# Two tiles in a step of a two-layer graph attention kernel, with the turned activations moved to the projection banks

## The reference

```python
def layer(x, adj, l):
    q, k, v = projections(x, l)                    # 384x384 each, float32
    if l == 0:
        s = q @ k.T / sqrt(32) + beta * adj        # -9e15 where adj <= 0
    else:
        s = q @ k.T * 384 ** -0.5 + adj            # a row that is all zero gives zero
    o = softmax(s) @ v
    return o if l == 0 else o @ Wo.T + bo
x = layernorm(x + layer(x, adj, 0))
x = layernorm(x + layer(x, adj, 1))
```

## Time and profile before

| | us |
|---|---|
| median of 3 runs | 1067.73 (1065.7 to 1071.74) |
| the profiled execution | 1066.61 |
| its span, first to last instruction | 1064.8 |
| PE busy | 1035.8 (97%) |
| DVE busy | 793.6 (75%) |
| POOL busy | 788.6 (74%) |
| ACT busy | 451.0 (42%) |
| chain that ended last | PE 89%, DVE 3%, POOL 3% |

### The profile page before, as it was taken

The page is one execution under the profiler, slowest core; times in us unless marked ns, Lnnn a source line. Parts: engine busy times, 40 slices in busy tenths (PEclk is TensorE's granted clock), DMA queues, the critical chain, the costliest instruction groups (busy, mean ns, idle before and its releaser), DMA issues.

```text
span 1064.8 us, 38493 instructions
## 1 busy us (share of the span) xinstructions
PE 1035.8 (97%) x16896; PEld 898.1 (84%) x16896; DVE 793.6 (75%) x1578; ACT 451.0 (42%) x717; POOL 788.6 (74%) x646
## 2 busy tenths in 40 slices
PE   6999999999999999999999999999999999999985
PEld 5888888888888888888888888888888888888874
DVE  3587886868778687786868778687786868877884
ACT  4454434444344443444445344443434444444332
POOL 1588777778687786877778777777877867777676
PEclk9999999999999999999999999999999999999998
DMA  6421112112111121111211021121111210010100
GB/s 205 142 71 52 34 44 66 40 44 62 40 44 39 44 62 44 40 46 39 67 44 52 33 59 39 44 62 44 39 47 36 62 44 10 17 37 10 35 32 31
DMA packets 61750, 53.33 MB, mean 50 GB/s; under 512 B 35984, under 2 KB 55440, under 8 KB 61584
## 3 DMA queue, kind: packets, MB, share of 16 engines
q1 hardware_dynamic: 60752, 49.69, 15.9%
q10 hardware_dynamic: 832, 1.18, 0.3%
HBM read 38.28 MB, written 12.58 MB: 48 GB/s over the span
## 4 chain that ended last, share of the span: by engine, by line
PE 89%; DVE 3%; POOL 3%; issue 2%; DMA 1%; ACT 1%; POOLq 0%; SPq 0%; DVEq 0%
PE ps_u L374 53%; PE ps_h L374 9%; PE ps_s L392 8%; PE ps_s L464 8%; PE ps_h L486 7%; PE ps_h L410 2%; PE ps_h L498 2%; POOL probs L806 1%; DMA xt_in<-in_x_t 1%; DVE row_sum L716 1%; ACT probs L597 1%; DVE probs L675 1%; DVE row_max L684 1%; POOL probs L812 0%; POOL xt_lo L832 0%
## 5 line engine op out<-in xcount | busy, mean ns | idle before, releaser
L806 POOL TENSOR_TENSOR probs<-probs,row_max 128x768 f32<-128x768 f32 x128 | 193.2, 1510 | 223.2 <-DVE row_max L684 223.2
L812 POOL TENSOR_TENSOR probs<-probs,row_inv 128x768 f32<-128x768 f32 x128 | 193.2, 1509 | 2.8 <-DVE row_inv L720 2.5
L716 DVE TENSOR_REDUCE row_sum<-probs 128x12 f32<-128x768 f32 x128 | 122.0, 953 | 68.0 <-ACT probs L597 68.0
L559 ACT COPY probs_t<-ps_s 128x768 f32<-128x768 f32 x128 | 102.8, 803 | 109.9 <-PE ps_s L464 109.8
L374 PE MATMUL ps_u<-w_hi_v,xt_lo 128*128 128x384 f32 x384 | 137.7, 359 | 0.0
L374 PE MATMUL ps_u<-w_hi_v,xt_hi 128*128 128x384 f32 x384 | 129.4, 337 | 0.0
L374 PE MATMUL ps_u<-w_lo_v,xt_hi 128*128 128x384 f32 x384 | 129.1, 336 | 0.0
L684 DVE TENSOR_REDUCE row_max<-probs 128x12 f32<-128x768 f32 x128 | 121.4, 948 | 2.2
L374 PE MATMUL ps_u<-xt_hi,w_lo_q 128*128 128x512 f32 x285 | 121.6, 427 | 0.0
L597 ACT ACTIVATE probs<-probs 128x768 f32<-128x768 f32 x128 | 108.6, 849 | 28.9 <-POOL probs L806 27.0
L374 PE MATMUL ps_u<-xt_hi,w_lo_k 128*128 128x512 f32 x288 | 118.2, 410 | 0.9 <-ACT q_sb L585 0.9
(11 more groups left out here) (80 smaller groups left out, 2102.6 us busy)
## 6 DMA issues: line engine op xcount, KB each, us to landing
x_in<-in_x SPq DMA_DIRECT2D x16, 768.0 KB, 4.6
out<-z SPq DMA_DIRECT2D x64, 192.0 KB, 1.9
xt_in<-in_x_t SPq DMA_DIRECT2D x15, 768.0 KB, 4.7
adj<-in_adj SPq DMA_DIRECT2D x64, 128.0 KB, 3.0
xt_in<-in_x_t SPq DMA_DIRECT2D x3, 256.0 KB, 4.4
q_sb<-in_wq ACTq DMA_DIRECT2D x3, 192.0 KB, 4.6
k_sb<-in_wk ACTq DMA_DIRECT2D x1, 576.0 KB, 7.4
v_sb<-in_wv SPq DMA_DIRECT2D x1, 576.0 KB, 7.3
```

The source lines that it names most:

```text
L559: nc.scalar.copy(probs_t[:].rearrange("p (a i) n -> p a (i n)", a=2), ps_s[:, 0:2, 0:KT * P]).then_inc(probs_t_ready, 1)
L716: nc.vector.reduce_sum(row_sum[p][:], probs[p][:].rearrange("p i b k -> p (i b) k"), AX_X)\
L806: nc.gpsimd.tensor_tensor(s, s, over_keys(row_max[p]), ALU.subtract).then_inc(shifted, 1)
L812: nc.gpsimd.tensor_tensor(s, s, over_keys(row_inv[p]), ALU.mult).then_inc(probs_ready, 1)
```

## The change

- `slots` lets the turns (phases) 2 to 27, 26 of the 32, run in two steps of two tiles; the others keep four steps of one. `cur`, `prev` and `last` are now groups of tiles, j being the place (0 or 1) in the group. `last` is still the group of two steps before, so it is now up to a turn back.
- Scores of the second tile go to the other half of the same ps_s banks; heads of the second tile to the next columns of ps_h; turned probabilities of tile j to banks 2j and 2j+1 of ps_s, and to a buffer `probs_t[j]` each; the result of tile j to bank j of ps_h. `probs` and the row statistics have four buffers instead of two.
- The turned activations are numbered among the units (kind "x", `columns`) and use the two ps_u banks. A step of layer 1 thus puts its early unit, two x units and its late units through the two banks.
- `heads_out` and `heads_lo` handle both tiles in one instruction.
- ACT, DVE and POOL have a new order in a step (below).
- The o1 weights are staged in the memory of adj1, without a staging buffer of their own; SP stores behind its loads.
- The first products: ten matmuls of the identity (`warm_up`), then `first_units`, two units at once, high by high first; the scores of the very first tile wait for one q and k unit at a time, and in phase -1 the early unit is copied out ahead of the activations.

```diff
+def slots(phase):
+    if 2 <= phase <= N_TURNS - 5:
+        return [(0, 1), (2, 3)]
+    return [(0,), (1,), (2,), (3,)] if phase < N_TURNS else [(0,), (1,)]
...
-UNIT_ORDER = [u for s in STEPS for u in s.units]
+UNIT_ORDER = [u for s in STEPS for u in early(s) + columns(s) + late(s)]
...
# PE
+            def bank_free(no):
+                if no > 2:
+                    freed = UNIT_ORDER[no - 3]
+                    if freed[2] == "x":
+                        pe.wait_ge(xt_lo_ready[1], low_no((*freed[:2], freed[3])))
+                        return
...
+            def turn_activations(unit):
+                layer, c, _, t = unit
+                no = UNIT_NO[unit]
+                pe.wait_ge(normed, at((0, c, t)) + 1)
+                bank_free(no)
+                for g in range(KT):
+                    last = nc.tensor.transpose(ps_u[:, (no - 1) % 2, g * P:(g + 1) * P],
+                                               x1[c % 3][:, t, g * P:(g + 1) * P], ident[:])
+                last.then_inc(unit_made, 1)
...
+            def warm_up():
+                for _ in range(WARM_UP):
+                    nc.tensor.matmul(ps_h[:, 0, 0:P], ident[:], ident[:], start=True, stop=True)
+            def first_units():
+                last = [None, None]
+                for g in range(KT):
+                    pe.wait_ge(first_hi, 2 * g + 2)
+                    for n in range(2):
+                        nc.tensor.matmul(ps_u[:, n, :], w_hi["q0"][:, g, n * P:(n + 1) * P], xt_hi[0][:, g, :],
+                                         start=(g == 0), stop=False)
+                    pe.wait_ge(first_lo, 2 * g + 1)
...
+            warm_up()
+            first_units()
             for s in STEPS:
-                if s.cur:
-                    scores(s.cur)
+                for j, tile in enumerate(s.cur):
+                    scores(tile, j, s)
                 for unit in early(s):
-                    make_unit(unit)
-                if s.last:
-                    result(s.last)
-                if s.turned:
-                    turn_activations(s.turned, s.last)
-                if s.prev:
-                    turn_probs(s.prev, s.cur)
+                    if UNIT_NO[unit] > 2:
+                        make_unit(unit)
+                for j, tile in enumerate(s.last):
+                    result(tile, j, s)
+                for unit in columns(s):
+                    turn_activations(unit)
+                for j, tile in enumerate(s.prev):
+                    turn_probs(tile, j, s)
                 for unit in late(s):
-                    make_unit(unit)
-                if s.prev:
-                    heads(s.prev, s.turned)
+                    if UNIT_NO[unit] > 2:
+                        make_unit(unit)
+                for j, tile in enumerate(s.prev):
+                    heads(tile, j, s)
...
# ACT
+                for unit in early(s):
+                    unit_out(unit)
                 if place == (-1, 1):
                     for t in range(TILES):
                         activations_hi((*ORDER[1], t))
-                for unit in early(s):
+                if s.phase >= 0:
+                    for tile in s.turned:
+                        activations_hi(tile)
+                for j, tile in enumerate(s.prev):
+                    probs_out(tile, j, s)
+                for tile in s.cur[:1]:
+                    exponentials(tile)
+                for unit in late(s)[:1]:
                     unit_out(unit)
...
+                for tile in s.cur[1:]:
+                    exponentials(tile)
+                for unit in late(s)[1:]:
+                    unit_out(unit)
...
# DVE
+                for j, tile in enumerate(s.cur):
+                    add_bias(tile, j, s)
+                for tile in s.cur[:1]:
+                    maxima(tile)
...
+                if s.phase >= 0:
+                    for tile in s.turned:
+                        activations_lo(tile)
+                for j in range(2):
+                    for tile in s.last[j:j + 1]:
+                        residual(tile, j)
+                    if len(s.ts) == 2:
+                        for unit in late(s)[j:j + 1]:
+                            unit_out(unit)
+                for tile in s.cur[1:]:
+                    maxima(tile)
+                for tile in s.cur[:1]:
+                    sums(tile)
+                for unit in late(s)[2 if len(s.ts) == 2 else 0:]:
+                    unit_out(unit)
+                for tile in s.cur[1:]:
+                    sums(tile)
...
# POOL
+                for tile in s.cur[:1]:
+                    shift(tile)
...
+                if s.phase >= 0:
+                    for tile in s.turned:
+                        add_bo(tile)
+                        activations_lo(tile)
+                for tile in s.cur[1:]:
+                    shift(tile)
+                for j in range(2):
+                    for tile in s.last[j:j + 1]:
+                        inverse_deviation(tile)
+                        normalise(tile)
+                    for tile in s.cur[j:j + 1]:
+                        scale(tile)
```

More of the change, by code:

```diff
@@ L36 @@
 FIRST_AT = [[0, 1], [2, 3], [4, 5], []]
-Step = namedtuple("Step", "phase t cur prev last done turned units")
+Step = namedtuple("Step", "phase ts cur prev last turned units")
 def at(tile):
@@ L56, in units_of_step, with columns @@
     return out
+def slots(phase):
+    if 2 <= phase <= N_TURNS - 5:
+        return [(0, 1), (2, 3)]
+    return [(0,), (1,), (2,), (3,)] if phase < N_TURNS else [(0,), (1,)]
 def schedule():
     steps = []
-    attended = {}
+    groups = [(), ()]
     for phase in range(-1, N_TURNS + 1):
[L63 to L70, removed]
+        for ts in slots(phase):
+            groups.append(tuple((*ORDER[phase], t) for t in ts) if 0 <= phase < N_TURNS else ())
+            turned = tuple((*ORDER[phase + 2], t) for t in ts) if phase + 2 < N_TURNS else ()
+            units = [u for t in ts for u in units_of_step(phase, t)] if phase < N_TURNS else []
+            steps.append(Step(phase, ts, groups[-1], groups[-2], groups[-3], turned, units))
     return steps
 STEPS = schedule()
+def columns(s):
+    return [(*tile[:2], "x", tile[2]) for tile in s.turned if tile[0] == 1]
 def early(s):
@@ L396, in scores @@
                 last.then_inc(scores_made, 1)
[L398 to L414, removed]
-                layer, c, kind, n = unit
-                p, no = home((layer, c)), UNIT_NO[unit]
+            def bank_free(no):
                 if no > 2:
                     freed = UNIT_ORDER[no - 3]
+                    if freed[2] == "x":
+                        pe.wait_ge(xt_lo_ready[1], low_no((*freed[:2], freed[3])))
+                        return
                     if freed[2] == "v" and freed[:2] == ORDER[-1]:
@@ L424, in make_unit @@
                         pe.wait_ge(qk_ready, QK_NO[freed])
+            def turn_activations(unit):
[7 more added lines that the diff above has]
+                last.then_inc(unit_made, 1)
+            def make_unit(unit):
+                layer, c, kind, n = unit
+                p, no = home((layer, c)), UNIT_NO[unit]
+                bank_free(no)
                 w = f"{kind}{layer}"
@@ L471, in heads @@
                 pe.wait_ge(probs_t_ready, at(tile) + 1)
-                if at(tile) > 0:
-                    pe.wait_ge(z_ready, at(tile))
-                if turned and turned[0] == 1:
-                    pe.wait_ge(xt_lo_ready[1], low_no(turned))
+                if s.last:
+                    pe.wait_ge(z_ready, at(s.last[-1]) + 1)
                 if (layer, c) == ORDER[-1]:
@@ L712, in sums @@
             def sums(tile):
-                layer, c, t = tile
-                p = t % 2
+                layer, c, p = tile
                 dve.wait_ge(exp_ready, at(tile) + 1)
@@ L802, in shift @@
             def shift(tile):
-                p = tile[2] % 2
+                p = tile[2]
                 pool.wait_ge(max_ready, at(tile) + 1)
@@ L817, in add_bo @@
                     return
-                pool.wait_ge(xt_made, second_no(tile))
+                pool.wait_ge(unit_made, UNIT_NO[layer, c, "x", t])
                 if second_no(tile) == 1:
```

241 lines of the change are left out of this document (116 added, 125 removed).

## The result

The changed kernel takes 1151.65 us (median of 4 runs, 1150.1 to 1158.42), the kernel before 1067.2 in the same measurements: a ratio of 1.080 with a 95% interval of 1.077 to 1.083. The forecast was 1081, with 1097 as the upper end of its range. The profiled execution took 1150.36 us, its span is 1148.4.

A forecast was written before the change was run, and what follows sets the result against it. The prediction took TensorE as the bound, busy 99.99 of 100 us. Pairs of turns added 15.6 and the start took off 2.0: 1066.6 + 15.6 - 2.0 = 1080.2, or 1081 for the median; range 1060 to 1097.

The forecast's parts named there:

- The seams: TensorE's changes of kind of work: two tiles share each, saving 0.47 us a step, 24 us over 13 pairs.
- a pair: Two turns, eight one-tile steps becoming four: 62.3 us of TensorE work, 65.6 with waits, against 64.4 before.
- The wait in A: TensorE waits 2.9 us for the fourth late unit's bank: 1.8 from the step's own chain, 1.1 from D's lateness.
- step A: Layer 1, tiles 0 and 1, with layer 0 results and four late q/k units: 15.6 us without waits.
- the two instructions that make the next bias, 1.2: VectorE's last work in D's chain, from 16.8 to 18.0, making VectorE enter A at 2.5 instead of 1.38.
- B: Layer 1, tiles 2 and 3, with four late v units: 13.6 us, no stall.
- C: Layer 0, tiles 0 and 1, with four late q/k units: 17.5 us, plus a 0.4 wait for GpSimd's second scale.
- D: Layer 0, tiles 2 and 3, with four late v units: 15.5 us, handing lateness on to A.
- The start: Warm-up products, new first-unit order and earlier evacuation: first scores about 2.6 us earlier, -2 us, bounds 0 and -4.
- rival 4: Seams not saved, or GpSimd's late second scale also delays C's fourth late unit: 1088 to 1105, chance 0.23.
- half the waits, 1.6 a pair: Part of the rival that TensorE is fed all the same (chance 0.10): waits of A and C halved, 1062.
- waits of 2.5 to 4 a pair: The forecast's own case for TensorE's waits over two turns: 1074 to 1088, chance 0.50.

The follow-up runs named there:

- the waits away: Changed kernel with heads before the last late unit, VectorE's second-tile maxima early and its order by layer, held v unit evacuated last: 1065.2 us, 0.997 of before.
- the kernel with single steps: The changed kernel with one tile in every step and all the rest of the change kept: 1064.8 us, 0.997 of before.
- heads first: The changed kernel with the heads of both tiles made before the last late unit in two-tile steps: 1098.4 us, 1.027 of before.
- scores twice: The kernel before, with TensorE making every tile's scores twice into the same place: 1190.3 us, 1.113 of before.
- 42 warm-up products: The changed kernel with 42 warm-up products instead of 10 at the front of TensorE's stream: 1156.6 us.
- the order mended: The 1065.2 us kernel (heads before last late unit, VectorE reordered, held v unit out last), plus step C's early unit between its two tiles' scores: 1058.0 us, 0.991.
- VectorE's maxima early: The changed kernel with the second tile's maxima ahead of both residuals and the first two v units on VectorE: 1116.7 us, 1.044 of before.

## Why the prediction was wrong

The sign was right, the size was not: +14 forecast, +84.5 measured, outside the range. The sign was not luck: the waits that the forecast reckoned are there, and without the stops the ledger below comes to about 1094, inside the range.

- **The seams: right.** 96 scores take 1.21 us to the next projection matmul (254.53 to 255.74), where two groups of 48 take 1.42; two heads groups take 1.17. No switch is paid between tiles. With the waits away a pair fell to 62.9, against 62.3 reckoned.
- **The wait in A: right in place, too small by 1.0.** The changed kernel, VectorE, GpSimd, ScalarE and TensorE in step A, which begins at 254.53:

```profile
256.35 1.84 DVE L688 SCALAR_TENSOR_TENSOR bias<-adj,beta_col,bias 128x512 f32<-128x512 f32 x1
258.12 1.94 DVE L717 TENSOR_TENSOR probs<-ps_s,adj_both 128x384 f32<-128x384 f32 x4
...
266.68 0.94 DVE L729 TENSOR_REDUCE row_max<-probs 128x12 f32<-128x768 f32 x1
```

```profile
256.00 1.64 POOL L873 TENSOR_TENSOR probs<-probs,row_inv 128x768 f32<-128x768 f32 x1
```

```profile
269.21 0.84 ACT L633 ACTIVATE probs<-probs 128x768 f32<-128x768 f32 x1 [3.67 <-POOL probs L867]
269.96 0.67 ACT L623 ACTIVATE k_sb<-ps_u,k_bias 128x512 f32<-128x512 f32 x1
```

```profile
260.20 0.85 PE L496 MATMUL ps_s<-ident,probs 128*128 128x128 f32 x6 [0.72 <-DVE probs L717]
...
261.87 0.55 PE L496 MATMUL ps_s<-ident,probs 128*128 128x128 f32 x3 [0.82 <-POOL probs L873]
...
270.68 0.50 PE L389 MATMUL ps_u<-xt_hi,w_lo_k 128*128 128x512 f32 x1 [1.79 <-ACT k_sb L623]
```

  The fourth late unit starts at 16.15 in A, released by ScalarE's evacuation behind the exponential; forecast was 15.15. VectorE began the bias of A at 3.6, not 2.5. The term that was off is "the two instructions that make the next bias, 1.2": the second took 1.84 us here, 0.82 in the mean of the earlier trace rows, which is 15 times 0.75 and once 1.84. Before the turned probabilities there are two waits where the forecast had one, of 1.45: 0.7 us for VectorE's bias and 0.8 for GpSimd's scale. A took 19.6 for 18.5; B, C and D 13.6, 17.7 and 15.4 for 13.6, 17.9 and 15.5.
- **The start: right.** The first scores come at 20.0 (23.2 before); turn 2 begins 1.8 us earlier, and the kernel with single steps is 0.3% faster than before, about 2 to 3 us.
- **The step that failed** is the sum itself: "Two tiles in a step go through each seam once" was costed as a gain only. I took the 0.01 us from one small matmul to the next as good for any length of the group. What the runs showed in its place: in and right behind a burst of 384 small instructions there are stops of 46.6 us, and the lower clock after them, for which the sum had no term. The ledger, from the step lengths of the two profiled executions (spans of 1148.4 and 1064.8, so 83.6 us):

| | us |
|---|---|
| 13 pairs at 66.3 instead of 64.4 | 25.4 |
| the 21 stops | 46.6 |
| the three shorter stops in the early unit | 2.5 |
| the lower clock | 17.1 |
| stops that fell into waits of TensorE, above all in A | -8.8 |
| the start | -1.8 |
| the last four turns, which were put at 0, within 2 (7.6, of which 4.9 are work that the turns of two-tile steps pass on) | 2.7 |

  The lower clock is read from single steps: the 11 steps B, C and D with a stretch of it are longer than an undisturbed one by their stop and by 1.0 to 1.6 us more (3.4 us at the lower clock, 8 steps) or 2.0 to 2.3 (6.8 us, 3 steps). Matmuls come 0.43 us apart there for 0.23. Steps B, C and D with a stop but the full clock are longer by the stop or less, at most 0.1 us more. A step A with a stop is longer by 0.5 to 1.8 us less than the stop, since TensorE would have waited there anyway.
- None of the four rivals had the fetch in it; rival 4 had the right direction with another cause. Two of their sums are off by 2 to 3 us by the prediction's own terms, and nothing hangs on it: half the waits, 1.6 a pair, make 1059 and not 1062, and waits of 2.5 to 4 a pair make 1071 to 1090 and not 1074 to 1088.

That the burst makes the stops is shown from both sides (heads first, scores twice) and by their places (42 warm-up products). That the thing waited for is the instruction fetch is read from the packets: at each of the 21 stops the number of packets that have landed fits the place in the stream, and TensorE goes on 1.2 to 1.6 us behind the end of the last one; at none of the 97 borders from the first stop to the last does it go on sooner. No run changed the fetch itself. The packets also show what makes a stop long: in the six stops of 2.8 to 3.6 us the packet began 0.4 to 0.9 us after TensorE had stopped, in the other fifteen 0.4 to 1.0 us before. Why it began late in those six is open.

## What to carry to other kernels

Count the instructions, not only the matmuls: where TensorE's stream has some 250 small instructions in less time than a fetch takes (an estimate from the run with the heads first: 3.2 to 3.4 us for 252 instructions still stopped it, 3.7 did not; with the scores twice it also stopped behind slower ones, where the packet began late), put a large matmul group in between, and look for stops with the releaser "issue" that come at equal distances in the stream. A bigger step doubles the chain of the other engines too: write down what stands behind each queue's second-tile instruction, and let units whose bank is wanted next leave first. When parts are merged, time the merged part alone before crediting its gain: here the same idea made 1151.7 and, with the order mended, 1058.0.

## What the runs showed of the hardware

- A burst of 384 weight loads and matmuls in 2.4 us outran the fetching of instructions: stops of 1.5 to 3.6 us at places 252 or 253 matmuls apart, each ended 1.2 to 1.6 us behind the last instruction packet, and a granted clock of 0.50 behind 12 of the 21, 51 us in the 26 turns.
- VectorE's `scalar_tensor_tensor` of two SBUF operands (L688, L645 before) took 0.75 us when it began during a GpSimd `tensor_scalar` and 1.84 us when it began during GpSimd's `tensor_tensor` of 768 columns, as at 256.35 above: that one had begun at 256.00 and ended at 257.64. So in 14 of its 16 executions in the changed kernel, and each time VectorE ended 0.55 us behind GpSimd. With VectorE's maxima early it falls beside the `tensor_scalar` in 13 of 16 and takes 0.75:

```profile
250.06 1.66 POOL L913 TENSOR_SCALAR z<-z,mean_var,rstd 128x384 f32<-128x384 f32 x1
251.03 0.75 DVE L688 SCALAR_TENSOR_TENSOR bias<-adj,beta_col,bias 128x512 f32<-128x512 f32 x1
```

  In the run with the heads first 12 of the 16 began during another GpSimd `tensor_tensor`, that of one column (`rstd`), and took 0.75 too, so it is not the kind of operation alone.

The Trainium skill, "SBUF — State Buffer", section Who interferes with whom, has a port pair that VectorE and GpSimd share, an exclusive lock, and has a VectorE instruction with two SBUF inputs contend with a GpSimd instruction that reads SBUF. The 1.84 us agree. The 0.75 us do not: beside a `tensor_scalar` of GpSimd, which reads SBUF as well, nothing was blocked, and here the measurement decides.
